# Two stages of a one-core kernel made into one: the tokens' first transform step and the filters' spectra

## The reference

```
t = _to_tokens(x)                                 # 4096 tokens of 128 channels per image
u = _ln_t(t)                                      # each token less its mean, by its deviation
Vf = rfft(phi, n=8192); Uf = rfft(u, n=8192)      # 16 filters, and the tokens
U_plus = irfft(Vf * Uf); U_minus = the same with alternating signs
out = sum over filters k of U_plus[k] @ Mpp[k] + U_minus[k] @ Mpm[k]
```

## Time and profile before

| what | value |
|---|---|
| median of 3 runs | 2967.88 us (2960.94 to 2973.62) |
| the profiled execution | 2962.64 us, of which the span of the trace is 2960.9 us |
| PE busy | 2353.1 us, 79% of the span |
| DVE busy | 1494.5 us, 50% |
| ACT busy | 1310.6 us, 44% |
| POOL busy | 301.9 us, 10% |
| mean granted TensorE clock | 0.901 |

### The profile page before, as it was taken

The page is one execution under the profiler, slowest core; times in us unless marked ns, Lnnn a source line. Parts: engine busy times, 40 slices in busy tenths (PEclk is TensorE's granted clock), DMA queues, the critical chain, the costliest instruction groups (busy, mean ns, idle before and its releaser), DMA issues. The chain is left out here.

```text
span 2960.9 us, 78991 instructions
## 1 busy us (share of the span) xinstructions
PE 2353.1 (79%) x34528; PEld 1793.6 (61%) x34528; DVE 1494.5 (50%) x3491; ACT 1310.6 (44%) x2623; POOL 301.9 (10%) x586
## 2 busy tenths in 40 slices
PE   0465889934534999999999999999877785789898
PEld 0334888822213888888888888888733652344444
DVE  6341343423341666666666555665511253377777
ACT  0463243425302666666656656665511264333332
POOL 0112111200020000000000000000012001022221
PEclk9765798967787999999999999999999697799999
DMA  6437455632353111111111111100088630000000
GB/s 196 126 113 117 86 102 99 116 128 114 133 126 103 43 43 43 43 43 43 43 43 43 43 43 40 42 21 18 23 267 277 223 93 13 5 23 23 24 21 28
DMA packets 183365, 235.04 MB, mean 79 GB/s; under 512 B 35820, under 2 KB 142825, under 8 KB 179513
## 3 DMA queue, kind: packets, MB, share of 16 engines
q1 hardware_dynamic: 150117, 120.85, 15.4%
q0 software_dynamic: 29024, 90.96, 11.5%
q10 hardware_dynamic: 3888, 18.25, 1.6%
HBM read 141.68 MB, written 88.31 MB: 78 GB/s over the span
## 5 line engine op out<-in xcount | busy, mean ns | idle before, releaser
L947 DVE COPY spc_g<-spc_pz 128x512 f32<-128x512 f32 x1024 | 629.0, 682 | 311.9 <-PE spc_pz L843 311.8
L917 ACT ACTIVATE spc_g<-spc_pz 128x512 f32<-128x512 f32 x1024 | 549.4, 612 | 284.4 <-PE spc_pz L843 284.0
L843 PE MATMUL spc_pz<-spc_v,spc_as 108*128 108x128 bf16 x8192 | 554.2, 219 | 16.6 <-issue 3.3
L843 PEld LDWEIGHTS spc_pz<-spc_v,spc_as 108*128 108x128 bf16 x8192 | 473.9, 97 | 105.3 <-ACT spc_g L917 32.7
L864 PE MATMUL spc_pz<-spc_g,spc_u 128*20 128x128 f32 x16384 | 469.1, 274 | 21.5 <-DVE spc_g L947 17.3
L864 PEld LDWEIGHTS spc_pz<-spc_g,spc_u 128*20 128x20 f32 x16384 | 451.1, 135 | 48.3 <-ACT spc_g L917 30.1
L1454 PE MATMUL moe_ex<-moe_ew,moe_d 128*128 128x512 f32 x512 | 249.9, 611 | 33.0 <-DVE moe_yt L1611 32.6
L828 PE MATMUL spc_pu<-spc_f,spc_s 128*128 128x256 f32 x768 | 207.5, 395 | 71.9 <-DMA spc_s<-s_sf 71.9
L1611 DVE SCALAR_TENSOR_TENSOR moe_yt<-moe_ex,moe_gb,moe_yt 128x128 f32<-128x128 f32 x768 | 209.7, 343 | 103.3 <-ACT moe_yt L1513 102.0
L501 DVE SCALAR_TENSOR_TENSOR inv_xo<-inv_pa,inv_mask,inv_xo 128x256 f32<-128x256 f32 x256 | 123.6, 484 | 228.8 <-PE inv_pa L459 167.4
L479 ACT ACTIVATE inv_b<-inv_pb 112x1024 f32<-112x1024 f32 x128 | 125.4, 1021 | 228.2 <-PE inv_pb L438 228.2
(11 more groups left out here) (201 smaller groups left out, 2231.0 us busy)
## 6 DMA issues: line engine op xcount, KB each, us to landing
s_yd<-spc_yo SPq DMA_DIRECT2D x128, 160.0 KB
s_sf<-fwd_so ACTq DMA_DIRECT2D x16, 1024.0 KB, 5.3
spc_s<-s_sf POOLq DMA_DIRECT2D x32, 512.0 KB, 6.4
ivs_y<-s_yd POOLq DMA_DIRECT2D x32, 512.0 KB, 5.2
s_td<-ivs_to SPq DMA_DIRECT2D x32, 512.0 KB, 4.7
ln_t<-s_td SPq DMA_DIRECT2D x32, 512.0 KB, 3.8
inv_x<-s_xn SPq DMA_DIRECT2D x88, 112.0 KB
inv_x<-s_xn POOLq DMA_DIRECT2D x88, 112.0 KB, 8.1
```

Source lines behind the costliest of these rows:

```text
L843: m = pe.matmul(pz[:, (p + 2) % 3, e // 4, 2 * FT * (e % 4):2 * FT * (e % 4) + 2 * FT], AS[:, x, 8 * p + e, :], V[:, k, x, :, FT * t:FT * ...
L917: act.activation(g_out(p, 0), g_in(p, 0), ACT.Copy).then_inc(ga, 1)
L947: v.tensor_copy(g_out(p, 1), g_in(p, 1)).then_inc(gd, 1)
```

## The change

`filters` goes away as a stage; its work is done inside `forward`. The loop is written out anew. In each of 8 turns (n) and 4 quarters (c), PE does the first step of quarter c of half image n, turns quarter c of half image n + 2, and after every second quarter makes one f of the filters. ACT empties `pf`, copies quarter c of n + 2 and normalises quarter c of n + 1. DVE empties its half, makes the statistics of quarter c of n + 2, and after every second quarter splits one f; the aggregation for n + 2 stands at the turn's end and the scales at the start of the next. `xt` has three buffers instead of two, `pt` two banks instead of four. The filters' product with `d1` is made first of all. The stores of `SF` and `SP` are issued by SP, behind the loads of images in its order; the loads and stores of the filters are issued by POOL.

```diff
-        xt = A.sb("xt", [P, 2, HH, 2, C])
+        xt = A.sb("xt", [P, 3, HH, 2, C])
-        pt = A.ps("pt", [P, 4, CH])
+        pv = A.ps("pv", [KX, 2, 2, 256])
+        pt = A.ps("pt", [P, 2, CH])
...
+            pool.wait_ge(sp_out, 32)
+            load(0)
+            load(1)
+            for f in range(NF1):
+                pool.wait_ge(parts_ready, f + 1)
+                for s in range(3):
+                    pool.dma_start(S["VS"][s, f].rearrange("k x c f -> k x (c f)"), parts[:, f % 2, s]).then_inc(outs[f % 2], 16)
+                if f + 2 < NF1:
+                    load(f + 2)
...
+            for n in range(NU):
+                if n < 2:
+                    load_image(n + 2)
+                for half, ready in ((0, so_a), (1, so_ready)):
+                    sp.wait_ge(ready, 4 * n + 6)
...
+                    sp.dma_start(dst[n // 2, n % 2], so[:, half, n % 2].rearrange("p h m -> p (h m)")).then_inc(s_out[n % 2], 16)
...
+            for n in range(NU):
+                for c in range(4):
+                    first_step(n, c)
+                    if n + 2 < NU:
+                        turn(n + 2, c)
+                    if c % 2:
+                        filters(2 * n + c // 2)
...
+            for n in range(NU):
+                for c in range(4):
+                    take(n, c)
+                    if n + 2 < NU:
+                        copy(n + 2, c)
+                    if n + 1 < NU:
+                        normalise(n + 1, c)
+                if n + 2 < NU:
+                    deviation(n + 2)
...
+            for n in range(NU):
+                if n + 1 < NU:
+                    scales(n + 1)
+                for c in range(4):
+                    take(n, c)
+                    if n + 2 < NU:
+                        statistics(n + 2, c)
+                    if c % 2:
+                        split(2 * n + c // 2)
+                if n + 2 < NU:
+                    aggregate(n + 2)
...
-STAGES = (prepare, first_mixer, forward, filters, spectrum, inverse, layer_one)
+STAGES = (prepare, first_mixer, forward, spectrum, inverse, layer_one)
```

More of the change, by code:

```diff
@@ L535, in forward @@
         f_done, so_ready, so_a = A.sem("f_done"), A.sem("so_ready"), A.sem("so_a")
-        s_out = [[A.sem(f"s_out{half}{k}") for k in range(2)] for half in range(2)]
+        loads = [A.sem(f"loads{k}") for k in range(2)]
+        outs = [A.sem(f"outs{k}") for k in range(2)]
+        v_done, chain, parts_ready, sp_out = A.sem("v_done"), A.sem("chain"), A.sem("parts_ready"), A.sem("sp_out")
+        s_out = [A.sem(f"s_out{k}") for k in range(2)]
         block = A.ctx.enter_context(nc.Block())
@@ L663, in body @@
-            def body(n, k, more, i):
-                if more:
-                    turn(n + 1, 1 - k, i + k)
-                pe.wait_ge(u_ready, n + 3)
-                for c in range(4):
-                    for half, free in ((0, so_a), (1, so_ready)):
-                        pe.wait_ge(free, 4 * n + c + 1)
-                        pe.matmul(pf[:, 2 * (c % 2) + half, :], d1[:, half * P:half * P + P],
-                                  u[:, k, 2 * c:2 * c + 2].rearrange("p h q c -> p (h q c)"),
-                                  start=True, stop=True).then_inc(f_done, 1)
@@ L674, in _, with turn @@
-            turn(0, 0, 0)
-            units(body)
-            for n in range(2):
+            def turn(n, c):
+                if c == 0:
+                    pe.wait_ge(x_in[n // 2 % 2], 16 * (n // 4) + 16)
+                if 4 * n + c >= 2:
+                    pe.wait_ge(xt_ready, 4 * n + c - 1)
+                for m4 in range(4):
+                    at = 16 * (n % 2) + 4 * c + m4
+                    m = pe.transpose(pt[:, c % 2, m4 * P:m4 * P + P],
+                                     x1c[:, n // 2 % 2].rearrange("c (q m) -> c m q", q=P)[:, at], ident[:])
+                m.then_inc(turned, 1)
@@ L712, in _, with filters @@
+            def filters(f):
                 k = f % 2
@@ L720, in _ @@
                 m.then_inc(v_done, 1)
+            pe.wait_ge(const_in, 48)
+            for n in range(2):
+                for half in range(2):
+                    pe.matmul(pf[:, 2 * n + half, 0:16 * KX], d1[:, half * P:half * P + P],
+                              ph[:, 8 * n:8 * n + 8, :].rearrange("p h m -> p (h m)"),
+                              start=True, stop=True).then_inc(f_done, 1)
+            for n in range(2):
+                for c in range(4):
+                    turn(n, c)
@@ L722, in _, with statistics @@
         @block.vector
         def _(v):
[L724 removed]
+            chained = [0]
             def step(ins):
[L727 removed]
+                chained[0] += 1
                 ins.then_inc(chain, 1)
[L729 to L731 removed]
+                v.wait_ge(chain, chained[0])
+            def statistics(n, c):
+                v.wait_ge(xt_ready, 4 * n + c + 1)
+                for t in range(4 * c, 4 * c + 4):
+                    m = v.bn_stats(st[:, n % 2, t, :], xt[:, n % 3, t // 2, t % 2, :])
+                m.then_inc(st_ready, 1)
@@ L732, in _, with take, split @@
+            def take(n, c):
+                if c == 0 and n >= 2:
+                    v.wait_ge(s_out[n % 2], 32 * (n // 2))
+                v.wait_ge(f_done, 8 * n + 2 * c + 6)
+                v.tensor_copy(so[:, 1, n % 2, 2 * c:2 * c + 2, :].rearrange("p h m -> p (h m)"),
+                              pf[:, 2 * (c % 2) + 1, :]).then_inc(so_ready, 1)
+            def split(f):
                 k = f % 2
```

232 lines of the change are left out of this document (94 added, 138 removed).

## The result

The changed kernel takes 2877.93 us (median of 4 runs, 2872.82 to 2893.51) against 2968.05 for the kernel before (4 runs, 2960.94 to 2973.62): a ratio of 0.9698, 95% interval 0.9655 to 0.974. It is 90 us faster. The forecast was 2858, so 20 us of the gain stayed away. The profiled execution took 2882.68 us with a span of 2880.8. In the same accounting as the prediction's (2962.64 less 106.8) it misses by 26.9.

The account below looks back on a forecast made before the run. `forward` was taken as bound by order, not by an engine. Ending the merged stage at 755.2 instead of 861.99 saves 106.8 us; 2962.64 becomes 2855.8, and half of a 5.2 us run offset gives 2858, range 2845 to 2889.

Parts of the forecast that it names:

- if PE waits for the table: Sign in the merged stage: the prediction is wrong if PE waits for the filters' table load, forecast to cost nothing.
- The sum of the turn: Merged loop, one half image and two filters: PE 12.6, DVE 13.6, ACT 11 us; 14.0 to 14.2 us a turn taken.
- the ring's 13.9: Merged loop: normalising 11.3 us behind aggregation, plus 16.5 us from first product to aggregation's end, 27.8 us over two turns.
- the landing of the filters' loads: POOL's table loads in the turns: landing taken as 4 us, at no cost; 17 us in all if 8.1.
- 8 + L over two f: Filters' load loop: split, six issues, landing L, products, split take 8 us plus L, against 14; L up to 6 free.
- Bytes ... a share of 0.65: no bound: Merged stage: 32 MB keep the DMA engines busy 88 us of some 135, so they do not bound it.
- The end: Last split to `spectrum`'s first issue: 3.04 us before, 0.7 us added because POOL issues the last stores.
- I cost their removal at nothing: ACT's two DMA issues go to SP; they lay in time ACT waited anyhow, so no gain was counted.
- Less overlap: Rival, chance 0.14: engines overlap less in the merged loop, turns of 16 to 19 us; 2879 us at 17, 2893 at 19.
- The lower clock: Rival, chance 0.05: PE stays at its lower clock in the merged stage, turns of 23.6 us, time 2929 us.
- Late loads: Rival, chance 0.03: loads through POOL land late, deciding from L = 20 us; with L = 24 the time is 2996 us.
- Better than the sum: Rival, chance 0.06: PE and DVE overlap at DVE's own 13.5 us and the start gains 2 us; 2848 us.

Follow-up runs that it names:

- the order alone: Changed kernel's new loop without the filters, which stay a stage of their own; both stages 193.8 us, median 2908.26 us, ratio 0.9805 to the kernel before.
- the four buffers: Changed kernel with four buffers instead of two for the filters' loads, first four tables issued ahead of the loop; stage 146.0 us, median 2879.4 us, ratio 0.9705.
- the small stores: Changed kernel writing only 256 of 2048 columns of each token store in the turns, whole buffers at the end; 2917.52 us, one run.
- that run: Changed kernel with the token stores issued by ACT at the end of its turn instead of SP; stage 156.0 us, 2866.51 us, one run.
- the four idle products: New order with filters as their own stage, plus four unread PE products at the end of every turn but the last; stages 180.2 us, 2901.7 us, one run.
- the best version: Changed kernel with no DMA by POOL: SP loads all 16 tables ahead and stores the filters; stage 141.6 then 140.3 us, ratios 0.9675 and 0.9654.

## Why the prediction was right and where it failed

**The number.** 2877.93 lies in the range of 2845 to 2889 and outside the forecast's own, 2848 to 2872. It is inside because the range had been widened for engines that overlap less and for an exposed store, and neither is what happened. By the prediction's own signs the mechanism failed in part: "if PE waits for the table" came true (7 waits, up to 4.1 us), the stage ended at 763.7 and not near 752, PE was busy 116.4 us at a clock of 0.89 where 125 above 0.9 was said. So the direction and the bound were understood, and that the time fell within the range is partly luck.

**What bounds: right.** The order was the bound and no engine. PE's 59.4 us of waits for `pf` went, and with the order alone the stages lost 54.4 us.

**The sum of the turn: right once its condition held.** PE 12.6, DVE 13.6 and the ring's 13.9 gave 14.0 to 14.2 a turn; the four buffers gave 13.91, PE 12.75 busy. The 0.2 a turn that was added was not there, and the ring's two parts were each off by 0.9, in opposite directions. DVE's 13.6 was too high: it was busy 11.96, 86% of the turn and not over 90%, since the sum had counted ACT's root and the pauses between a split's steps as DVE's.

**The step that failed: the landing of the filters' loads.** "By size the table's 256 KB is nearest to the 3.2, so I take 4 and no cost." It landed in 7.1 at the median and up to 10.1, and cost 16 us. With the same account of the loop, 8 + L over two f, an L of 7.2, 10.1 and 9.0 gives turns of 15.2, 18.1 and 17.0 us; measured are 14.75, 19.05 and 18.16. The mechanism and its price stood in the prediction ("at 8.1 it is 2 us a turn, 17 in all"); the size of L was wrong. It was chosen by the transfer's own size, where the runs showed that what else is in flight decides: 3.5 us with the small stores, 7.1 with 2 MB stored in each turn. The step "Bytes ... a share of 0.65: no bound" failed with it. The mean share was in fact 0.57, and a mean says nothing of the 2 MB bursts behind which a small load waits. The 2.6 us estimated from the Trainium skill ("DMA: Bandwidth & Descriptors", Anatomy of one DMA) is near the 3.1 to 3.2 of a transfer with the engines to itself and has no term for others' bytes.

**The end: failed by 8.1 us.** "Between nothing and the whole 1.5 us on top I take 0.7." The issues were not the cost. POOL's share in ending the stage grows with the DMAs that it issued in it, 96 here: 7.88 us of drain. The rows chosen from before could not show that, since POOL issued none in the two stages; the end of `first_mixer`, with its 13.59 us, could.

**The stores' move to SP, "I cost their removal at nothing": failed**, by 8 to 11 us on one run's evidence. ACT had the time, as said. What was not asked is where the 2 MB land in the turn once they go out earlier. It is part of the 16 us of the ring (119.8 in that run, 128.5 and 127.8 in the changed kernel) and does not come on top.

**The filters cost next to nothing against the order alone, for a reason that was not given.** A turn is 13.91 us with them and 13.8 without: they fill a gap in which PE would stand and lose its clock. So the change is 54.4 us by the order and 27 to 30 by the merging, and 52 to 54 by the merging when neither fault is there (193.8 less 141.6 or 140.3). Part of that is the clock: the order with the four idle products takes 180.2 us and turns of 12.14, so against an order that keeps its clock two filters cost 1.8 us a turn, and the repaired merging is worth 39 to 40.

**The rivals.** Less overlap (0.14): its time of 2879 came about, its mechanism did not, since turns of 13.91 need full overlap. The lower clock (0.05): fell; 0.95 from 639 to 760 us, and what it lost was behind the waits for the table. Late loads (0.03): L never reached the 20 us from which they would decide, and yet this was the mechanism that cost the most; it was treated as all or nothing. Better than the sum (0.06): only by 1 us, in the best version. That POOL's issues might stand still for two of DVE's instructions did not show: its six issues for an f take 3.34 us (653.15 to 656.49), as drawn.

**What stays open.** Why the drain at the end of `spectrum` is short for its 156 DMAs. What made the table land in 9.0 us in the second long turn, which came in the changed kernel's second trace too (18.13 us). Why the stages behind took 6.4 us more in the profiled execution while those ahead took 5.0 less; both lie in the blur between runs. Whether the stores' later issue or their queue is what helps on ACT.

## What to carry to other kernels

When a load gets two buffers, take its landing time from the company it will keep, not from its size: ask which megabytes are issued in the same turn, and if they are there, load ahead or add buffers, which here was worth 18 to 21 us of stage. Before POOL is given DMAs because it is idle, count them: it pays 0.08 us for each again behind its last instruction of the stage, and all engines wait for that unless POOL is done well ahead of them. When two stages are merged, run the order without the merging as well, for the work that seems to come free may be what keeps PE's clock up.

## What the hardware showed that was not expected

A stage in which POOL issued DMAs keeps all engines still at its end: POOL's drain took 3.96 us with 48 DMAs, 7.88 with 96 and 9.86 with 120, with DMA engines at a share of 0.01 and nothing else busy. It was the same for loads and stores in turns as for stores alone, and for DMAs that had been issued 1.3 or 21.7 us before. Only at the end of `spectrum` was it shorter, 5.6 to 5.9 us with 156. From the last issue of the block to POOL's next instruction that makes 2.0 us where ACT had issued the stores, 6.0 with 48 by POOL and 9.9 with 96.

A 256 KB load takes 3.2 us by itself, and 7.2 when it is issued 0.6 us behind 2 MB of stores from another engine's queue (9.0 and 10.1 were seen too); with the stores cut to an eighth the median is 3.5. A wait of 4.08 us of PE makes the f behind it take 3.32 us instead of 1.90. And four unread products a turn, 0.06 us of PE's busy time more (10.62 against 10.56), took 1.7 us off the turn by keeping the granted clock at 1.00.
